# Segment maxima of three softmax passes in two levels: scans within tiles, then across tiles

## The reference, cut to what matters

```python
# first layer, twice: 4 heads of 64, self loops added
e = al_s[src] + al_d[dst]
e = jnp.where(e > 0, e, NEG_SLOPE * e)
m = jax.ops.segment_max(e, dst, num_segments=n)
ee = jnp.exp(e - m[dst])
s = jax.ops.segment_sum(ee, dst, num_segments=n)
alpha = ee / (s[dst] + 1e-16)
out = jax.ops.segment_sum(alpha[:, :, None] * feat[src], dst, num_segments=n)
# third layer: one head
mx = jnp.maximum(jax.ops.segment_max(scores, tgt, num_segments=N), -1000000000.0)
ex = jnp.exp(scores - mx[tgt])
se = jax.ops.segment_sum(ex, tgt, num_segments=N)
```

## Time and profile before

| | us |
|---|---|
| runs | 5288.44, 5303.44, 5304.99, median 5303.44 |
| the profiled execution | 5288.36, span 5286.6, mean granted clock 0.924 |
| busy, share of the span | PE 4453.9 (84%), DVE 4204.5 (80%), POOL 3107.9 (59%), ACT 2974.0 (56%) |
| first softmax pass | first scan at 1492.0, last at 2193.0 |
| second softmax pass | first scan at 2306.6, last at 2907.1 |
| third softmax pass | first scan at 3870.6, last at 4304.1 |

### The profile page before, as it was taken

One profiled execution on the slowest core, in us unless ns is written; L12 is line 12 of the kernel. 1 busy time (PEld: TensorE's weight loads), 2 busy tenths in 40 slices (PEclk: granted clock), 3 DMA queues, 4 the chain that ended last, 5 costly groups with the idle time before them and its releaser, 6 DMA issues. The chain is left out here.

```text
span 5286.6 us, 75793 instructions
## 1 busy us (share of the span) xinstructions
PE 4453.9 (84%) x21191; PEld 3335.9 (63%) x21191; DVE 4204.5 (80%) x12564; ACT 2974.0 (56%) x7552; POOL 3107.9 (59%) x2813
## 2 busy tenths in 40 slices
PE   3999999999958888858888699999957757988887
PEld 3888888888736666636666456666634436765555
DVE  5999999999868888769999368888868878975554
ACT  2999999999914444414444357677745544431111
POOL 3676666666267676343333277777544426647777
PEclk9999999999979999968889899999978878999998
DMA  4888888888734444247777446555557766654444
GB/s 137 299 313 310 310 311 309 309 309 310 281 117 127 127 132 128 87 141 248 264 270 254 149 141 184 184 179 181 170 169 253 258 223 183 206 161 134 150 148 132
DMA packets 645561, 1096.74 MB, mean 207 GB/s; under 512 B 82230, under 2 KB 465654, under 8 KB 645021
## 3 DMA queue, kind: packets, MB, share of 16 engines
q1 hardware_dynamic: 525866, 837.50, 46.0%
q0 software_dynamic: 119168, 253.97, 16.1%
q10 hardware_dynamic: 112, 0.40, 0.0%
HBM read 523.88 MB, written 575.95 MB: 208 GB/s over the span
## 5 line engine op out<-in xcount | busy, mean ns | idle before, releaser
L1398 POOL DMA_INDIRECT got<-F,index x392 | 504.3, 1286 | 504.9 <-PE acc L1548 400.2
L850 PE MATMUL mm<-w,tt 128*128 128x264 f32 x3136 | 733.0, 387 | 2.6 <-ACT tt L894 2.6
L850 PEld LDWEIGHTS mm<-w,tt 128*128 128x128 f32 x3136 | 582.7, 191 | 93.1 <-ACT tt L894 2.8
L1557 ACT ACTIVATE rows<-acc 128x260 f32<-128x260 f32 (+1 forms) x588 | 227.4, 387 | 559.8 <-PE acc L1548 559.8
L1544 PE MATMUL acc<-got,sel 128*128 128x260 f32 (+1 forms) x1176 | 425.3, 449 | 99.2 <-DVE sel L1519 93.3
L816 POOL DMA_INDIRECT place<-PLACE,place_ix x392 | 413.3, 1054 | 119.4 <-issue 119.4
L2692 DVE SCALAR_TENSOR_TENSOR agg<-mask,agg,acc 128x128 f32<-128x128 f32 x784 | 247.9, 344 | 253.5 <-PE acc L2679 140.6
L850 PE MATMUL mm<-wl,tt 128*128 128x264 f32 x1568 | 411.7, 385 | 0.7 <-ACT tt L894 0.7
L788 POOL DMA_INDIRECT xd<-in_x_dram,index x196 | 224.6, 1146 | 316.7 <-DMA XD<-xd 285.1
L1287 PE MATMUL kv<-wkv,ht 128*128 128x512 f32 x784 | 378.4, 606 | 0.1
L1548 PE MATMUL acc<-rows,carry 128*128 128x260 f32 (+1 forms) x1008 | 349.2, 431 | 8.3 <-ACT rows L1557 1.9
(11 more groups left out here) (391 smaller groups left out, 13339.6 us busy)
## 6 DMA issues: line engine op xcount, KB each, us to landing
F<-f1o SPq DMA_DIRECT2D x97, 528.0 KB
F<-f2o SPq DMA_DIRECT2D x97, 528.0 KB
HL<-ho SPq DMA_DIRECT2D x97, 528.0 KB
xin<-in_x_dram SPq DMA_DIRECT2D x97, 512.0 KB, 5.8
H<-h SPq DMA_DIRECT2D x97, 512.0 KB, 3.3
X<-x3o SPq DMA_DIRECT2D x97, 512.0 KB, 3.5
out_dram<-oo SPq DMA_DIRECT2D x97, 512.0 KB
drow<-DSTF SPq DMA_DIRECT2D x84, 448.0 KB
```

Of the source, the lines that this page charges most:

```text
L850: last = nc.tensor.matmul(mm[PAIR[stage, q]][:, r, 0:F2W], lhs[:, q, 2 * r + k, :], w[:, k, :], start=(k == 0), stop=(k == KB - 1))
L1398: nc.gpsimd.indirect_dma_start(out=buf[:, n % SLOTS, t, :], out_offset=None, in_=table, in_offset=bass.IndirectOffsetOnAxis(ap=index[:, n ...
L1557: nc.scalar.activation(self.rows[:, n % 2, t, :], self.acc[tile % 2][:, 0:self.width], ACT.Copy)\
```

## The change

The 7 tiles of `top`, now stored head by head, are turned by one transpose: heads x 7 partitions (28 or 7), 128 edges along the free dimension. The scans run within a tile, 128 elements on 28 partitions, both started from -1e30. So that maxima cross tiles, the first and last value of each partition are multiplied with the identity into two diagonal matrices (`edges`), and two products with a matrix of ones spread these ends to all 128 partitions (`ends`); one transpose brings the maxima within the tiles back. `differences` then runs two scans of 8 x heads elements (32 or 8) over the ends on all partitions, with penalties `across_tiles` that are made once ahead of the first pass, adds `beyond` (0 for an edge whose segment reaches over the tile's edge, -1e30 for others), takes the maximum of both sides and of the tile's own, subtracts, and takes the ratio from the scans. ScalarE copies the last value of a group into `ends` for the next group, behind the exponent (semaphore `past`). `pen` has a layout of its own for each direction and head: 2 x heads DMAs a group. The calls of `differences` get the argument `link`; line 2514 writes `top[:, 0, :]`.

```diff
-                    nc.tensor.matmul(ps_c[:, 0:T], last_row[:, :], dst_col[:, :], start=True, stop=True)\
-                        .then_inc(s_pe, 1)
+                    nc.tensor.matmul(ps_c[:, 0:T], last_row[:, :], dst_col[:, :], start=True, stop=True)
+                    nc.tensor.matmul(ps_c[:, 256:256 + T], ident[:, 0:1].to_broadcast([P, P]), dst_col[:, :],
+                                     start=True, stop=True).then_inc(s_pe, 1)
...
+                    V.memset(first_of[:, T:T + 1], -1.0)
+                    V.tensor_copy(first_of[:, 0:T], ps_c[:, 256:256 + T])
...
+        beyond = sb("beyond", [P, 2, T])
+        across_tiles = sb("across_tiles", [P, NS, 2, HQ * 8])
...
-                self.pen = self.sb("pen", [H, 2, SE + 1])
-                self.fwd = self.sb("fwd", [H, SE])
-                self.bwd = self.sb("bwd", [H, 2, SE])
+                C = H * GS
+                self.pen = self.sb("pen", [C, 2, 2, P])
+                self.fwd = self.sb("fwd", [C, P])
+                self.near = self.sb("near", [C, P])
+                self.edges = self.sb("edges", [C, 2, C])
+                self.ones = self.sb("ones", [C, P])
+                self.over = self.sb("over", [P, 2, 40])
+                self.far = self.sb("far", [P, 2, H, GS])
+                self.peak = self.sb("peak", [P, H, GS])
...
-                self.back = self.ps("back", [P, GS + 1, H])
+                self.back = self.ps("back", [P, 128])
+                self.near_t = self.back[:, 0:C].rearrange("p (h t) -> p h t", h=H)
+                self.ends = self.back[:, 64:64 + 16 * H].rearrange("p (k h t) -> p k h t", k=2, h=H)
...
             def start_dve(self, dve, link):
+                V = nc.vector
+                V.memset(self.ends[:, 0, :, 0], -BIG)
+                link(V.memset(self.ends[:, 1, :, GS], -BIG))
                 dve.wait_ge(self.done["start"], 1)
-                link(nc.vector.tensor_scalar(self.less[:, :], ident[0:self.h, 0:self.h], -1.0, None, ALU.mult))
-                dve.sem_inc(self.done["start"], 1)
...
             def penalties(self, sp, n):
                 hold(sp, self.done["most"], n - 1, None)
-                sp.dma_start(self.pen[:, n % 2, :], PEN[n * SE:(n + 1) * SE + 1].partition_broadcast(self.h))\
-                    .then_inc(self.pen_in[n % 2], 16)
+                for k in range(2):
+                    for h in range(self.h):
+                        sp.dma_start(self.pen[h * GS:(h + 1) * GS, n % 2, k, :],
+                                     PEN[n * SE + k:(n + 1) * SE + k].rearrange("(t p) -> t p", p=P))\
+                            .then_inc(self.pen_in[n % 2], 16)
...
-                V.tensor_tensor(self.top[:, :, :], self.lg[:, :, 0, :], self.lg[:, :, 1, :], ALU.max)\
-                    .then_inc(self.done["top"], 1)
+                V.tensor_tensor(self.top[:, :, :].rearrange("p h t -> p t h"), self.lg[:, :, 0, :], self.lg[:, :, 1, :],
+                                ALU.max).then_inc(self.done["top"], 1)
...
             def turn_scores(self, pe, n):
                 hold(pe, self.done["top"], n + 1, None)
                 hold(pe, self.done["most"], n, None)
-                for t in range(GS):
-                    last = nc.tensor.transpose(self.turned[0:self.h, t * P:(t + 1) * P], self.top[:, t, :], ident[:, :])
-                last.then_inc(self.done["turned"], 1)
+                nc.tensor.transpose(self.turned[0:self.h * GS, 0:P], self.top[:, :, :].rearrange("p h t -> p (h t)"),
+                                    ident[:, :]).then_inc(self.done["turned"], 1)
             def segment_most(self, dve, link, n):
-                V, H, s = nc.vector, self.h, n % 2
-                hold(dve, self.pen_in[s], 16 * (n // 2 + 1), None)
+                V, C, s = nc.vector, self.h * GS, n % 2
+                hold(dve, self.pen_in[s], 32 * self.h * (n // 2 + 1), None)
                 hold(dve, self.done["turned"], n + 1, None)
-                hold(dve, self.done["most"], n, None)
+                link(V.tensor_tensor_scan(self.fwd[:, :], self.pen[:, s, 0, :], self.turned[0:C, 0:P], -BIG,
+                                          ALU.add, ALU.max))
                 hold(dve, self.done["back"], n, None)
-                link(V.tensor_tensor_scan(self.fwd[:, :], self.pen[:, s, 0:SE], self.turned[0:H, 0:SE],
-                                          self.bwd[:, 1 - s, SE - 1:SE], ALU.add, ALU.max))
-                V.tensor_tensor_scan(self.bwd[:, s, ::-1], self.pen[:, s, 1:SE + 1][:, ::-1], self.fwd[:, ::-1], -BIG,
-                                     ALU.add, ALU.max).then_inc(self.done["most"], 1)
+                link(V.tensor_tensor_scan(self.near[:, ::-1], self.pen[:, s, 1, ::-1], self.fwd[:, ::-1], -BIG,
+                                          ALU.add, ALU.max))
+                V.tensor_tensor(self.edges[:, :, :], ident[0:C, 0:C].unsqueeze(1).to_broadcast([C, 2, C]),
+                                self.near[:, ::-(P - 1)].unsqueeze(2).to_broadcast([C, 2, C]), ALU.mult)\
+                    .then_inc(self.done["most"], 1)
                 self.make_way(dve)
...
             def turn_back(self, pe, n):
-                H, s = self.h, n % 2
+                C = self.h * GS
                 if n == 0:
-                    pe.wait_ge(self.done["start"], 2)
+                    pe.wait_ge(self.done["start"], 1)
                 hold(pe, self.done["most"], n + 1, None)
                 hold(pe, self.done["diff"], n, None)
-                for t in range(GS):
-                    nc.tensor.transpose(self.back[:, t, :], self.bwd[:, s, t * P:(t + 1) * P], ident[0:H, 0:H])
-                nc.tensor.matmul(self.back[:, GS, :], self.bwd[:, 1 - s, SE - 1:SE].to_broadcast([H, P]),
-                                 ident[0:H, 0:H], start=True, stop=False)
-                nc.tensor.matmul(self.back[:, GS, :], self.bwd[:, s, 0:1].to_broadcast([H, P]),
-                                 self.less[:, :], start=False, stop=True).then_inc(self.done["back"], 1)
-            def differences(self, dve, n):
+                nc.tensor.matmul(self.ends[:, 0, :, 1:GS + 1], self.ones[:, :], self.edges[:, 0, :], start=True, stop=True)
+                nc.tensor.matmul(self.ends[:, 1, :, 0:GS], self.ones[:, :], self.edges[:, 1, :], start=True, stop=True)
+                nc.tensor.transpose(self.back[:, 0:C], self.near[:, :], ident[0:C, 0:C]).then_inc(self.done["back"], 1)
+            def reach(self, k):
+                first = 39 * k
+                flat = self.over[:, :, :].rearrange("p k x -> p (k x)")
+                return flat[:, first:first + 8 * self.h].rearrange("p (h t) -> p h t", h=self.h)
+            def differences(self, dve, link, n):
                 V, H, K = nc.vector, self.h, self.kinds
                 hold(dve, self.done["back"], n + 1, None)
-                hold(dve, self.done["top"], n + 1, None)
+                hold(dve, self.done["past"], n, None)
+                flat = self.over[:, :, :].rearrange("p k x -> p (k x)")
+                ends = self.back[:, 64:64 + 16 * H]
+                V.tensor_tensor_scan(flat[:, 0:8 * H], across_tiles[:, n, 0, 0:8 * H], ends[:, 0:8 * H], -BIG,
+                                     ALU.add, ALU.max)
+                link(V.tensor_tensor_scan(flat[:, 39:39 + 8 * H][:, ::-1], across_tiles[:, n, 1, 0:8 * H][:, ::-1],
+                                          ends[:, 8 * H:16 * H][:, ::-1], -BIG, ALU.add, ALU.max))
+                beside = self.over[:, :, 0:8 * H].rearrange("p k (h t) -> p k h t", h=H)[:, :, :, 0:GS]
+                k = link.go(V.tensor_tensor(self.far[:, :, :, :], beside,
+                                            beyond[:, :, n * GS:(n + 1) * GS].unsqueeze(2).to_broadcast([P, 2, H, GS]),
+                                            ALU.add))
+                before, here = self.reach(0)[:, :, 0], self.reach(1)[:, :, 0]
+                if H == 1:
+                    V.tensor_scalar(self.ratio(n), before, here, 0.0, ALU.subtract, ALU.min)
+                else:
+                    r = link.go(V.tensor_tensor(self.ratio(n), before, here, ALU.subtract))
+                link.need(k)
+                k = link.go(V.tensor_tensor(self.peak[:, :, :], self.far[:, 0, :, :], self.far[:, 1, :, :], ALU.max))
+                if H > 1:
+                    link.need(r)
+                    V.tensor_scalar(self.ratio(n), self.ratio(n), 0.0, None, ALU.min)
+                link.need(k)
+                link(V.tensor_tensor(self.peak[:, :, :], self.peak[:, :, :], self.near_t, ALU.max))
                 V.tensor_tensor(self.weights(n), self.lg[:, :, :, :],
-                                self.back[:, 0:GS, :].unsqueeze(2).to_broadcast([P, GS, K, H]), ALU.subtract)
-                V.tensor_scalar(self.ratio(n), self.back[:, GS, :], 0.0, None, ALU.min).then_inc(self.done["diff"], 1)
+                                self.peak[:, :, :].rearrange("p h t -> p t h").unsqueeze(2).to_broadcast([P, GS, K, H]),
```

(17 more changed lines are left out.)

17 lines of the change are left out of this document (9 added, 8 removed).

## The result

The changed kernel takes 5264.88 us (median of 4 runs, 5260.79 to 5268.81), the kernel before in the same comparison 5301.23 (5288.44 to 5304.99). The ratio is 0.9936, with a 95% interval of 0.9916 to 0.9955: 36 us less. The profiled execution of after took 5268.8 us, its span 5267.0; that of before 5288.4 and 5286.6, so this pair is only 19.6 apart.

A forecast was written before the change was run, and what follows sets the result against it. It took TensorE with ScalarE to bound the first pass, loops through all three engines the others. First pass -29, second -8 and -3, third +11, setup +0.5: -29 us, forecast 5274 us; own range -16 to -65, bounds -81 to +27.

The forecast's parts named there:

- 0.72 for the forward transposes: First pass: one transpose instead of seven saves 0.72 us a group, 90% at the full and 10% at the half clock.
- VectorE has slack: First pass: the loop is TensorE with ScalarE; VectorE waits 1.4 us a group for rows, so it does not bound.
- On the path: nothing in a steady group: Scans, all passes: VectorE's 3.1 us less a group shortens no steady group, since the scans lie beside TensorE's work.
- VectorE is the bound after all: Rival, all passes: each group gains 1.8 us with four heads, 2.2 with one; 157 us, 5146 us; chance 7%.
- 4 x 0.3 and 3: Second pass, first groups: 0.3 us each as in every group, plus 3 us because nothing runs beside the scans there.
- the new wait: Second pass: VectorE reaches the differences sooner and waits there for TensorE's back, 1 to 3 us a group.
- Chain 0.85 forecast: Third pass, differences with one head: the linked short instructions add 0.85 us a group, between 0.5 and 1.6.
- `turn_back` -0.3: Third pass: the shorter transposes back save 0.3 us a group, because the last pass's own latency stays.
- Forward transposes -0.3: Third pass: only 0.3 of 1.45 us a group is gained, because the first product would then wait for sel.
- The clock is the term: Third pass: more of the products falls to the half clock; 0.15 us a group lost, within 0 to 0.55.
- The rival of the clock: Second and third pass: half clock lasts one more tile a group, +51 us, together +22, 5325 us; chance of slower 14%.
- the rival of a dearer chain: Differences, second and third pass: 0.35 us a step costs 31 us, total 5303; within 0.3%, this way or mixed, 23%.

The follow-up runs named there:

- scans_beside: The changed kernel with five more scans of 128 elements a group on VectorE behind the two of segment_most, in all three passes; 5296.97 us, ratio 0.9992.
- busy_scans: The changed kernel with idle products in TensorE's waits in all passes, and five more scans of 128 elements a group on VectorE; 5252.10 us, ratio 0.9919.
- chain_before: The kernel before with four more linked 7-element instructions at the head of differences in the third pass; 5313.79 us, ratio 1.0040.
- six_turns_first: The changed kernel with six more transposes of top a group behind the real one in the first pass; 5321.09 us, ratio 1.0034.

## Why the prediction was right, and where it was not

I forecast 5274 us, -29 us from before; it is 5265, -36, inside the forecast's own range. The three passes of the profiled pair gave -30.4, where the sum had -29. Step by step:

- **First pass, -1.09 a group forecast, -1.41 measured; the reason was half of it.** The sum was built from TensorE's stream alone: 0.72 for the forward transposes and 0.37 for those back. Added up over TensorE's timelines, from each instruction's start to the next one's, that stream did lose 1.05 at the forward transposes (1.20 us a group before, 0.15 after), 0.35 at `turn_back` and 0.14 of the wait for the second scan, and 0.13 came back elsewhere. The 0.72 was too small because it took 10% of the transposes at the half clock, by the mean clock of the pass, where 15 of 23 groups have them there in whole or in part. The step that failed is "VectorE has slack", and with it "On the path: nothing in a steady group": VectorE's loop stood at 25.5 us (with the clock held), 0.6 below the mean group, and held TensorE up in 8 groups of 23. Without its relief the forward and backward transposes together bring 0.27 (scans_beside). The rival "VectorE is the bound after all" had 1.8 us a group for this relief. With the clock held the pass gained 1.72, but not from that alone: the next loop, TensorE's, would have stopped it at some 24.65 us, had the transposes stayed. That a term which was too small and a floor which was left out came close to the measured sum is luck.
- **First groups.** The first four periods of the first pass gained 7.4 us, where I had 4 x 1.09; those of the second 5.4 for 4 x 0.3 and 3.
- **Second pass, -0.3 forecast, -0.28 measured.** VectorE idles 52.7 us in 23 times ahead of its first scan in `differences`, where I had put the new wait; the view names no engine that ended it. scans_beside confirms that the scans are beside other work in this kernel; busy_scans suggests that this is so because TensorE's products are partly at the half clock. That the 0.28 is `turn_back`'s, as the sum had it, was not tried, and the granted clock fell by 0.02 meanwhile.
- **Third pass, +0.4 forecast, +0.77 measured.** Chain 0.85 forecast, 0.89 measured. `turn_back` -0.3, measured -0.37. Forward transposes -0.3, measured -0.11, for the product waits 0.96 us for `sel`; the way to the next `turned` brought 0.12 more, of which chain_before, with all its transposes, has 0.08 too. The clock is the term that was mis-sized: 0.15 within 0 to 0.55, where the seven tiles measured 0.47 more.
- **The rival of the clock** had the right place and the wrong cause and size: I let it follow from the longer gap, and chain_before shows no loss from that. In the second pass the granted clock fell from 0.89 to 0.87 and the group was 0.28 us shorter all the same.
- **The chain's price** held, so the rival of a dearer chain did not come. Its own sum has a slip: it says that the second pass gives back its 0.3 and loses as much, which is 0.6 a group, and adds 0.4; with 0.6 it would be 36 us and not 31. VectorE's busy time fell by 168 us, where I had 150.

## What to carry to other kernels

A wait of the busiest engine is slack only so far as nothing that it waits for depends on its own lateness: follow the wait of the third engine too (here ScalarE's for the exponent, ahead of the copies in its queue), and look which instruction of TensorE's queue stands in wait for VectorE. Look at the groups one by one, and not at their mean: here two loops less than 1 us apart took turns, and taking work from TensorE alone gained little. To learn which engine bounds a loop, give time back to one engine at a time; where the clock of TensorE moves, hold it first and check in the table of stretches that it is held, since otherwise 0.7 us of work can cost 2.2. And when a chain of short instructions replaces a long one, ask in each loop whether the long one was on the path: in the one-head pass it was not, and the old form is better there.

## What the runs showed of the hardware

- Idle products in TensorE's waits took some 100 us off the changed kernel (ratio 0.9936 to 0.9740) and 76 off the kernel before (5299.45 to 5223.24). The granted clock went from 0.95, 0.87 and 0.79 to 1.00, 1.00 and 0.95.
- Six transposes cost 0.55 us a group with the clock held and 2.2 without: in six_turns_first TensorE's clock stood at 0.89 over the pass, and its periods settled at 27.3 us, where after has three of 23.76 and one each of 26.42 and 25.17 in turn.
- In the third pass of before the clock rose 2.6 to 5.7 us after TensorE's first transpose (the last slow product started 2.3 to 4.9 us after it), with nothing changed in the work or in the wait before it.
- A scan of 896 elements takes 2.06 us, of 128 elements 0.40, of 32 elements 0.20, of 8 elements 0.17. The number of partitions made no difference (896 elements on 4 and on 1: 2.06; 128 on 28 and on 7: 0.40; on 98: 0.41), and reading PSUM hardly any (128 elements 0.40 from PSUM, 0.41 from SBUF).
